# Issuing the DMA transposes of the one-hots from ScalarE, at the start of its step, instead of from SyncE

## The reference, cut to what matters

```python
y = einsum('nchw,dc->ndhw', gn(x), Wp) + bp      # 512 channels: 8 heads x (32 point + 32 value)
# per head and per quarter of the image (a region of 64 x 64 pixels): 64 centres, means of 8 x 8 pixels
sim = sigmoid(alpha * cos(x_point, c_point) + beta)
max_v, max_i = sim.max(axis=2), sim.argmax(axis=2)            # best centre of each pixel
agg = cat_c.at[idx].add(mv[:, None] * cat_x)                  # scatter: pixels summed into their centre
agg = agg[:, :-1] / agg[:, -1:]
disp = mv[:, None] * agg[idx]                                 # gather: each pixel gets its centre back
x = x + einsum('nchw,dc->ndhw', disp, Wm) + bm
```

## Time and profile before

| | us |
|---|---|
| median of 3 runs (lowest to highest) | 4887.37 (4882.97 to 4894.53) |
| the profiled execution | 4887.86 |
| its span in the trace | 4886.0 |
| busy in the span: TensorE | 4551.5 (93%) |
| VectorE | 3976.0 (81%) |
| ScalarE | 3214.3 (66%) |
| GpSimd | 3182.8 (65%) |
| share of the 16 DMA engines, transposes and all | 66% on the hardware queue |

### The profile page before, as it was taken

How to read it: one execution, slowest core, us unless ns; L and a number is a source line. 1 busy time by engine, 2 the same in 40 slices (tenths; PEclk the granted TensorE clock), 3 DMA queues, 4 the chain that set the end, 5 groups by cost and what they waited for, 6 DMA issues and landing times.

```text
span 4886.0 us, 147006 instructions
## 1 busy us (share of the span) xinstructions
PE 4551.5 (93%) x55888; PEld 4483.8 (92%) x55888; DVE 3976.0 (81%) x8662; ACT 3214.3 (66%) x8171; POOL 3182.8 (65%) x3423
## 2 busy tenths in 40 slices
PE   1899999999999999999999999999999999999950
PEld 0899999999999999999999999999999999999940
DVE  3788899988888888888888888888888878888730
ACT  4666677767777677776767767776776666666521
POOL 1455666677776776767767677776767777767630
PEclk9999999999999999999999999999999999999975
DMA  5444455677777777776777777777777756666438
GB/s 169 107 120 127 115 125 124 145 178 174 186 182 184 173 180 184 182 185 168 185 187 182 174 177 186 183 185 165 184 185 183 173 146 153 154 151 156 115 108 201
DMA packets 1852784, 799.19 MB, mean 164 GB/s; under 512 B 1663008, under 2 KB 1663408, under 8 KB 1852080
## 3 DMA queue, kind: packets, MB, share of 16 engines
q1 hardware_dynamic: 1852080, 789.77, 66.1%
HBM read 395.15 MB, written 260.05 MB: 134 GB/s over the span
## 4 chain that ended last, share of the span: by engine, by line
PE 88%; DMA 2%; SPq 2%; issue 2%; POOL 2%; ACT 1%; DVE 1%; POOLq 1%; ACTq 0%
PE bank L1016 59%; PE bank L1094 9%; PE bank L1116 7%; PE bank L1168 7%; PE bank L1147 4%; DMA chunk<-x 1%; SPq L345 1%; DMA out<-fin 1%; POOL dl L640 0%; POOL xl L621 0%; POOL vals L636 0%; PE bank L1044 0%; SPq L314 0%; SPq L327 0%; ACT ysq L805 0%
## 5 line engine op out<-in xcount | busy, mean ns | idle before, releaser
L621 POOL TENSOR_TENSOR xl<-xr,xh 128x512 fp32r<-128x512 f32 x512 | 655.8, 1281 | 939.2 <-ACT xh L814 928.4
L636 POOL TENSOR_TENSOR vals<-vals,vpart 128x528 f32<-128x528 f32 x512 | 612.1, 1195 | 249.0 <-ACT vpart L824 249.0
L792 ACT ACTIVATE yh<-bank,bpf 128x256 fp32r<-128x256 f32 x1024 | 428.6, 469 | 513.8 <-PE bank L1016 511.9
L910 DVE TENSOR_REDUCE rank<-bank 128x8 f32<-128x512 f32 x1024 | 687.0, 686 | 32.7 <-PE bank L1016 11.3
L640 POOL TENSOR_TENSOR dl<-dsq,dh 128x512 fp32r<-128x512 f32 x512 | 657.6, 1284 | 63.3 <-ACT dsq L820 63.3
L583 POOL TENSOR_TENSOR vpart<-vals,vpart 128x528 bf16<-128x528 f32 x512 | 612.9, 1197 | 96.3 <-ACT vpart L762 94.4
L928 DVE TENSOR_TENSOR hot<-bank,rank 128x512 bf16<-128x512 f32 x1024 | 652.9, 676 | 0.0
L1016 PE MATMUL bank<-xh,wph 128*128 128x256 f32 x2048 | 620.6, 303 | 21.5 <-POOL xl L621 13.9
L1016 PE MATMUL bank<-dh,wmh 128*128 128x256 f32 x2048 | 624.6, 305 | 3.6 <-POOL dl L640 3.6
L1016 PE MATMUL bank<-ch,yh 128*128 128x256 f32 x2048 | 621.8, 304 | 0.0
L962 DVE SCALAR_TENSOR_TENSOR yl<-bank,bpf,yh 128x256 fp32r<-128x256 f32 x1024 | 448.4, 479 | 196.7 <-ACT ysq L805 196.5
(11 more groups left out here) (167 smaller groups left out, 13738.6 us busy)
## 6 DMA issues: line engine op xcount, KB each, us to landing
chunk<-x SPq DMA_DIRECT2D x512, 256.0 KB, 3.9
xr<-x SPq DMA_DIRECT2D x1024, 128.0 KB, 2.5
mixed<-xr SPq DMA_DIRECT2D x480, 256.0 KB, 2.6
fin<-mixed SPq DMA_DIRECT2D x480, 256.0 KB, 3.7
out<-fin SPq DMA_DIRECT2D x960, 128.0 KB, 3.4
hot_t<-hot SPq DMA_TRANSPOSE x1024, 2.5
out<-xr SPq DMA_DIRECT2D x64, 128.0 KB, 2.8
wraw<-wp_t SPq DMA_DIRECT2D x1, 512.0 KB, 5.3
```

What stands on the lines that cost most here:

```text
L621: pool.tensor_tensor(xl[:, G0 % 2], xr[:, G0 % SLOTS], xh[:, G0 % 2].bitcast(F32), ALU.subtract).then_inc(s_xl, 1)
L636: pool.tensor_tensor(vals[:, G2 % 2], vals[:, G2 % 2], vpart[:, 0], ALU.subtract).then_inc(s_r1, 1)
L792: op = nc.scalar.activation(yh[:, m], y_ps[:, m], ACT.Identity, bias=b[:, m:m + 1])
L910: op = V.tensor_reduce(rank[:, t], sims[t], axis=AX.X, op=ALU.max)
```

## The change

The function `transpose_hot` moves from SyncE's list to ScalarE's, with its waits, and is called first in ScalarE's step. It was called first in SyncE's step. The first hunk below is in SyncE's loop, the second in ScalarE's list; the old function, which differs by `sp` for `act` and for `nc.scalar`, is taken out.

```diff
             for i in range(STEPS):
-                if on(i - 3):
-                    transpose_hot(i - 3)
                 if AHEAD <= i + AHEAD < NG:
                     load_x(i + AHEAD)
...
+            def transpose_hot(G):
+                act.wait_ge(s_g, upto(G - HOTS))
+                act.wait_ge(s_te[G % 4], upto(G // 4 - 1, 16 * TILES))
+                for t in range(TILES):
+                    act.wait_ge(s_hot[t], upto(G))
+                    nc.scalar.dma_start_transpose(hot_t[:, G % HOTS, :, t * P:(t + 1) * P], hot[:, G % 2, t]
+                                           ).then_inc(s_te[G % 4], 16)
+
             for i in range(STEPS):
                 G0, G1, G2, G3, J1 = i, i - 1, i - 2, i - 3, i - GATHER
+                if on(i - 3):
+                    transpose_hot(i - 3)
                 if on(G2):
                     act.wait_ge(s_nc, upto(G2))
                     nc.scalar.activation(lnn[:, :], rnorm[:, G2 % 2], ACT.Ln, scale=LN_SCALE)
```

More of the change, by code:

```diff
@@ L320, in store_mixed @@
                 sp.dma_start(tmp[J], xr[:, J % SLOTS].rearrange("p k f -> p (k f)")).then_inc(s_tmp[J % 4], 16)
[L322 to L328, removed]
             def band_groups(n, b):
```

## The result

| | before | after |
|---|---|---|
| median | 4885.17 us (4 runs) | 6656.94 us (6643.74 to 6687.27, 4 runs) |
| ratio, 95% interval | | 1.363 [1.3608, 1.3652] |
| span of the profiled execution | 4886.0 us | 6655.9 us |
| mean granted clock of TensorE | 0.976 | 0.889 |

The change costs 1772 us. I had forecast 6034 us with a range of 5880 to 6420: the direction was right, the size too small by 623 us, and the result lies outside the range.

What follows compares the result with a forecast made beforehand. TensorE was taken as the bound before, a ring through the transposes after. Steps 21 to 514 +1008, steps 3 to 20 +17, the last pair +3, two queues +118: +1146 on 4888 gives 6034 us, range 5880 to 6420.

Steps and rivals of the forecast that it cites:

- the ring: Gather, transposes, ScalarE's front half, `yl`, norms, similarities, next gather: no slack, 10.12 us a step, 10.73 with a square.
- the pair: A step's two transpose issues on ScalarE: 2.51 us, with a forecast range of 2.5 to 3.0.
- The two waits of TensorE: Norms would wait for `yl` about 1 us a step, 500 us in all; the scatter for `vpart` 0.9.
- The parts of the ring at full clock: Start-to-start times from the earlier trace, including 2.40 us for norms and similarities and 0.90 from gather to transposes.
- a rival at 8%: TensorE's clock drops as it idles; TensorE needs 13 us a step: about 7200 us, 6600 if half the time; 8%.
- The second way: Cross-check from today's 8.81 us step plus ScalarE's 4.6 us delay, less idle time regained: 10.7 to 11 us a step.
- The rival's own sign: A granted clock of TensorE under 0.95 in the middle stretches would show the clock drop.
- 754 to `yh`: ScalarE's front: 0.50 us from line 754 to the chunk square, 0.61 a square, 0.57 from `vpart` to `yh`.
- the collision: Issues on two queues delay each other: 0.24 us a step, +118 us in the sum; as rival 0.7, 6261 us, 25%.
- `yl` to the norms: Ring part from `yl` on VectorE to the norms on TensorE, with TensorE idle and waiting: 1.02 us.
- steps 3 to 20: No gather to wait for, ScalarE itself the limit: 8.9 us a step against 7.98, +17 us.
- SyncE's freed time: Removing the transposes frees 2.5 us a step on SyncE; costed at nothing.

Runs made afterwards that it cites:

- e1: Kernel before, transposes still on SyncE, with ScalarE only waiting first in its step for that step's gather: 4947.44 us, ratio 1.0119.
- e2: Transposes first in ScalarE's step, but 19 one-hot buffers and 3 chunk buffers, so the wait is for the previous step's gather: 5045.07 us, ratio 1.0312.
- e5: Changed kernel with the transposes called behind `xh` in ScalarE's step instead of first: 4901.34 us, ratio 1.0032.
- e7: Changed kernel with TensorE's gather moved ahead of the 12 similarities, behind the norms: 5534.30 us, ratio 1.1329.
- e4_warm: Changed kernel with extra unused matmuls on TensorE, 6 ahead of the scatter and 3 ahead of the norms: 6284.76 us, ratio 1.2848.
- e6: Changed kernel with SyncE waiting at the start of its step until ScalarE's two transposes have landed: 6500.41 us, ratio 1.3307.

## Why the prediction was wrong

- **What bounds, and the ring: right.** The wait moved to ScalarE and holds the pair in every step from 21 on, the chain shows each link in my order, and e1, e2, e5 and e7 exclude the simpler causes. The two waits of TensorE came out at 512 us for the 500 I had put and 530 us for 0.9 a step, 444.
- **The parts of the ring at full clock: right.** 10.12 and 10.73 us were added from steps 3 and 4 of the trace of before; e4_warm gives 2.42 for 2.40 and 0.94 for 0.90, and `yh` to `ysq` to `yl` are within 0.01.
- **The step that failed: the sum has no term for the clock.** I carried the norms, similarities and the gather at full clock and put the clock into a rival at 8%, "against it: the gaps are short". In the trace they measure 3.05 + 1.18 us for 2.40 + 0.90. That is 0.93 x 493 = 458 us of the 623. In the turn shown TensorE idles 1.46 us before the scatter and 0.86 us before the norms, and the similarities behind that gap run at 1.2 GHz: 2.62 us from the first to the gather, where the next turn takes 1.52. The clock is low for 1195 us of the 6000 between 300 and 6300, a fifth, but it is low behind the idle time, and behind the idle time lies the part of TensorE's work that is in the ring: of the 1200 us at the low clock from step 21 on, 1025 fall on norms, similarities and gather, which take only a third of the time. The stretch at 1.00 with 58% busy in the earlier trace rows misled me; the one at 0.64 with 66% busy had gaps of the same size as the changed kernel now has, and its gather took 1.44 us instead of 0.87 (TensorE's timeline before):

```profile
4682.50 1.44 PE L1116 MATMUL bank<-tab,hot_t 128*128 128x64 bf16 x24 [1.31 <-ACT dsq L820]
4684.72 1.11 PE L1147 MATMUL bank<-ident,gath 128*128 128x128 f32 x4 [0.78 <-DVE gath L915]
```

  The next gather there, at 4689.71, had the same 1.31 us ahead of it and took 0.86, so such a gap is not followed by the low clock each time.

- **The second way was no check on this.** Its 10.7 to 11 us a step also took TensorE at the clock of before.
- **The rival's price was built wrongly too.** I took it as TensorE becoming the bound with 13 us a step. It never did, it is 79% busy after: a low clock costs through the ring alone, long before TensorE is full. The rival's own sign, a granted clock under 0.95 in the middle, did come (0.90). That its 6600 us for half the time at the low clock lies near the measured 6657 is luck: the clock was low for a fifth of the time, and the path was another.
- **754 to `yh`: 1.98 for 1.81, 84 us.** 0.15 of it lies between lines 754 and 756. It is 0.44 us from start to start in every run that has the pair just ahead, and 0.29 in e1_wait_only, where ScalarE has waited too and issued nothing. The drain of line 755 stands there, and its own record is longer, first in the changed kernel, then in e1_wait_only (line 757 there), then the start times in e1_wait_only:

```profile
L755 ACTq DRAIN  x512: 198/377/386, 125.6 to 6379.1; - x171
```

```profile
L757 ACTq DRAIN  x512: 218/233/236, 129.4 to 4677.2; - x171
```

```profile
3001.44 0.22 ACT L756 ACTIVATE lnn<-rnorm 128x16 f32<-128x16 f32 x1 [2.19 <-PE bank L1118]
3001.73 0.31 ACT L758 ACTIVATE rnorm<-lnn,cols 128x16 f32<-128x16 f32 x1
```

- **The pair: 2.84 for 2.75, 44 us.** Nearly right by two errors that cancel. The mean of a pair on SyncE before was already 2.74 us from the first start to the second end, with no second queue beside it, while I took the usual row of 2.51; the changed kernel adds 0.10 to that, and the collision is 0.15 when measured against e6, not 0.24. The Trainium skill, "Perfetto Trace Analysis", section "DMA Instruction — HWDGE", says that the sequencers share one generator and lock it; the runs agree in kind (2.69 apart, 2.84 together), but the full price of waiting for a whole issue, 0.7 us or more a step, is not there.
- **`yl` to the norms, 25 us, and steps 3 to 20**, 26 us more instead of 17. With the items above, 458 + 84 + 44 + 25 + 9 = 620 of the 623.
- **SyncE's freed time: right**, worth nothing; SyncE waits 4051 us for groups to store.

## What to carry to other kernels

Before an issue is moved to an engine with idle time, follow what the issue waits for: if that comes, through any other engine's list, from the work that now stands behind it, the step becomes the length of the ring, however idle the engine is on average. The place in the list decides, not the engine: behind `xh` the same 1024 issues cost 16 us, first in the step 1772. And once a ring leaves TensorE idle in each step, price the ring's part on TensorE at both clock levels from the start.

## What was not expected of the hardware

- A DMA issue on ScalarE can begin before the activation ahead of it has begun (3010.62 against 3010.74 in e2), so that about 0.8 us of that pair was hidden under the activations.
- A drain on ScalarE just behind DMA issues costs 0.15 us more than behind a plain wait (line 754 to 756: 0.44 us in the changed kernel, 0.29 in e1).
- With DMAs issued from two queues side by side, landing took nearly twice as long (transposes 4.7 us against 2.5, x loads 4.3 against 2.4 to 2.5), although the total rate was lower (124 GB/s in the middle, about 180 before). Nothing waited for it here: the trace books 231 us of idle time before line 754 to the landing of the transposes, 46 times, but every pair began right behind the gather.
